# A four-layer modulated-convolution and adapter kernel: each engine's instructions of a step are written in another order

## What is computed

```python
def cond(x, style, weights, biases, mod_w, mod_b):   # four convolutions, three taps each
    for i, typ in enumerate(('same', 'upsample', 'same', 'downsample')):
        s = style @ mod_w[i].T + mod_b[i]
        weight = SCALE * w * s[:, None, :, None]                      # per sample
        weight = weight * lax.rsqrt(jnp.sum(weight * weight, axis=(2, 3)) + EPS)[:, :, None, None]
        x = conv(x, weight) + b                                       # with a blur where sampled
```

## The kernel before

| piece (function) | TensorE tiles | fed by |
|---|---|---|
| filter halves (`pe_halves`) | ps<-gu_hi,mid_hi | DVE `gu_lo` |
| first convolution (`pe_first`, one per sample q) | ps<-x_hi,first_hi | ACT `x_hi` L381, DVE `x_lo` L626 |
| filter (`pe_filter`) | ps<-fb_hi,up_hi | ACT `fb_hi` L371, DVE `fb_lo` L620 |
| folded convolution (`pe_conv`, one per sample) | ps<-xp_hi,filt | the filter, ACT/DVE `filt`, and two transfers per sample that shift it to other partitions (L322, L323) |
| transposes of y (`pe_transpose_y`) | ps<-ident,y_nat | ACT `y_nat` |
| projection (`pe_project`, L1409) | ps<-proj,y_f | ACT `y_f` |
| big product in halves (`pe_ffn`, not in layer 0) | ps<-w_hi,y_hi | ACT `y_hi`, DVE `y_lo` |
| transpose of z (`pe_project_T`, L1429), tail (`pe_tail`) | ps<-ident,z_sb; ps<-tail_hi,zt_hi | DVE `dve_route`; ACT/DVE `zt_hi`, `zt_lo` L1391 |

## Time and profile before

### The profile page before, as it was taken

One profiled execution on the slowest core, in us unless ns is written; L12 is line 12 of the kernel. 1 busy time (PEld: TensorE's weight loads), 2 busy tenths in 40 slices (PEclk: granted clock), 3 DMA queues, 4 the chain that ended last, 5 costly groups with the idle time before them and its releaser, 6 DMA issues.

```text
span 2215.3 us, 28460 instructions
## 1 busy us (share of the span) xinstructions
PE 1924.8 (87%) x9806; PEld 1579.7 (71%) x9806; DVE 906.0 (41%) x2626; ACT 635.7 (29%) x1161; POOL 82.4 (4%) x140
## 2 busy tenths in 40 slices
PE   1877888866899999998589999999988999999977
PEld 1666666655777778777478888888776788877755
DVE  4334444454333333334444344434554333333234
ACT  0033444422332332221433222222143333332200
POOL 0000000000000000000000000000000000000000
PEclk9979999986999999998689999999988999999975
DMA  6144546432322333223522221222132222222226
GB/s 106 46 93 106 144 102 146 114 86 68 70 67 53 78 78 78 66 57 71 113 46 74 74 54 56 74 74 54 49 119 46 74 74 74 74 74 73 64 86 246
DMA packets 248777, 182.99 MB, mean 83 GB/s; under 512 B 197688, under 2 KB 207960, under 8 KB 248734
## 3 DMA queue, kind: packets, MB, share of 16 engines
q1 hardware_dynamic: 212878, 169.77, 29.8%
q10 hardware_dynamic: 31360, 10.56, 2.0%
q0 software_dynamic: 4496, 2.12, 1.1%
HBM read 108.99 MB, written 44.04 MB: 69 GB/s over the span
## 4 chain that ended last, share of the span: by engine, by line
PE 69%; issue 10%; DVE 9%; ACT 5%; DMA 3%; ACTq 2%; SPq 1%; DVEq 0%; POOL 0%; POOLq 0%
PE ps L789 56%; PE ps L1409 3%; PE ps L916 2%; PE ps L868 2%; ACT x_hi L381 2%; DVE w_lo L1163 1%; ACTq L1233 1%; DVE x_lo L626 1%; SPq L998 1%; DMA out_x<-raw 1%; DMA x_in<-in_L_ffn_kernel 1%; DMA raw<-in_x 1%; ACT w_hi L1056 1%; PE ps L1276 1%; ACT tail_hi L1306 1%
## 5 line engine op out<-in xcount | busy, mean ns | idle before, releaser
L789 PE MATMUL ps<-xp_hi,filt 128*128 128x512 f32 x1024 | 340.9, 415 | 15.4 <-DMA filt<-filt 15.4
L789 PE MATMUL ps<-w_hi,y_hi 128*128 128x512 f32 x768 | 316.9, 413 | 0.0
L789 PE MATMUL ps<-w_hi,y_lo 128*128 128x512 f32 x768 | 309.9, 404 | 0.0
L789 PE MATMUL ps<-w_lo,y_hi 128*128 128x512 f32 x768 | 308.9, 402 | 0.0
L789 PEld LDWEIGHTS ps<-xp_hi,filt 128*128 128x128 f32 x1024 | 192.3, 196 | 57.4 <-DMA filt<-filt 15.8
L789 PE MATMUL ps<-xp_lo,filt 128*128 128x512 f32 x512 | 205.5, 401 | 0.0
L643 DVE SCALAR_TENSOR_TENSOR filt<-ps,mods_pair,filt 128x256 fp32r<-128x256 f32 x128 | 56.1, 480 | 326.4 <-ACT filt L398 326.4
L789 PEld LDWEIGHTS ps<-w_lo,y_hi 128*128 128x128 f32 x768 | 148.2, 193 | 36.2
L398 ACT ACTIVATE filt<-ps,mods_pair 128x256 fp32r<-128x256 f32 x128 | 53.7, 471 | 411.8 <-PE ps L789 411.8
L789 PEld LDWEIGHTS ps<-w_hi,y_hi 128*128 128x128 f32 x768 | 148.9, 194 | 32.1
L789 PEld LDWEIGHTS ps<-w_hi,y_lo 128*128 128x128 f32 x768 | 148.3, 193 | 31.5
(11 more groups left out here) (315 smaller groups left out, 3271.3 us busy)
## 6 DMA issues: line engine op xcount, KB each, us to landing
x_in<-x_state SPq DMA_DIRECT2D x96, 256.0 KB, 4.0
x_res<-x_state SPq DMA_DIRECT2D x48, 512.0 KB, 3.9
x_state<-x_res SPq DMA_DIRECT2D x48, 512.0 KB, 2.9
filt<-filt SPq DMA_DIRECT2D x128, 128.0 KB, 2.7
filt<-filt SPq DMA_DIRECT2D x128, 96.0 KB, 2.4
raw<-in_x SPq DMA_DIRECT2D x16, 512.0 KB, 5.1
x_res<-in_x SPq DMA_DIRECT2D x16, 512.0 KB, 6.0
x_state<-raw SPq DMA_DIRECT2D x16, 512.0 KB, 5.1
```

Source lines behind the costliest of these rows:

```text
L789: ins = nc.tensor.matmul(out, st[x0], mv[x1], start=first and t == 0, stop=last and t == 2, **kw)
```

## The change

The same work is done; only its places in the engines' lists move, and the split of the matrix is done in halves. TensorE's step gets a version of its own for layer 0 (`pe_step_0`). The z transposes go to PSUM bank 6 instead of 7. The diff, cut:

```diff
         def sp_step(sp, l, i, j, more, load_next):
-            if l == 0 and j == 0:
-                load_kernel(sp, i)
             sp.dma_start(x_res[:, j, :], ...).then_inc(res_loaded[j], 16)
+            if more and load_next:
+                sp_load_x(sp, l, n + 3)
+            if l == 0 and more and j == 1:
+                load_kernel(sp, i + 1)
             if more:
                 sp_shift_filter(sp, l, n + 2)
-            if more and load_next:
-                sp_load_x(sp, l, n + 3)
...
         # ACT, layer 0: y_nat q0, x_hi, exp, fb_hi, half a kernel split, y_nat q1, filt, xp_hi q0, zt_hi, xp_hi q1
         # ACT, layers 1 to 3:
+            if l > 0 and more:
+                act_halves(act, l, n + 2, j)
                 act_split_x(act, l, n + 2, j)
             if l == 1 and j == 0:
                 split_mixed_act(act, i)
-            if more:
-                act_halves(act, l, n + 2, j)
...
         # DVE, layer 0, behind y_nat q0:
+                if more:
+                    dve_split_x(dve, l, n + 2, j, (0,))
                 dve_route(dve, l, n)
+                if more:
+                    dve_split_x(dve, l, n + 2, j, (1,))
+                    dve_halves(dve, l, n + 2, j)
+                if edges:
+                    dve_edge(dve, l, i + 1, 2)
+                if more:
+                    split_kernel_dve(dve, i, j)
...
+        def pe_step_0(pe, i, j, more, one_more):
+            pe_transpose_y(pe, l, n, one_more)
+            pe_conv(pe, l, n + 1, 0)
+            pe_edge(pe, l, i + 1, 1)
+            pe_project(pe, l, i, j)
+            pe_halves(pe, l, n + 2)
+            pe_edge(pe, l, i + 1, 2)
+            pe_conv(pe, l, n + 1, 1)
+            pe_filter(pe, l, n + 2)
+            pe_edge(pe, l, i + 1, 3)
+            pe_first(pe, l, n + 2, 0)
+            pe_project_T(pe, l, i, j)
+            pe_first(pe, l, n + 2, 1)
+            pe_edge(pe, l, i + 1, 4)
+            pe_tail(pe, l, i, j)
...
         def pe_step(pe, l, i, j, more, one_more):   # layers 1 to 3
+            pe_transpose_y, pe_conv 0, pe_edge 1, pe_conv 1, pe_halves, pe_edge 2, pe_project, pe_ffn 0,
+            pe_first 0, pe_edge 3, pe_first 1, pe_filter, pe_edge 4, pe_project_T, pe_ffn 1, pe_tail
...
-        def split_kernel_dve(dve, e):
-            dve.wait_ge(s["kernel_act"], e + 1)
+        def split_kernel_dve(dve, e, half):
+            dve.wait_ge(s["kernel_act"], 2 * e + half + 1)
```

More of the change, by code:

```diff
@@ L424, in act_step @@
             if l == 0 and j == 0 and not more:
-                split_kernel_act(act, i)
+                for half in range(2):
+                    split_kernel_act(act, i, half)
             if more:
@@ L621, in dve_halves, with dve_split_x @@
                                                ALU.mult, ALU.subtract).then_inc(s["dve_b"], 1)
-        def dve_split_x(dve, l, k, par):
-            for q in range(2):
+        def dve_split_x(dve, l, k, par, samples=(0, 1)):
+            for q in samples:
                 dve.wait_ge(s["act_x"], smp(l, k, q))
@@ L725, in dve_step @@
             if l == 0 and j == 0 and nxt:
-                split_kernel_dve(dve, i)
-                dve.wait_ge(s["kernel_dve"], 9)
+                for half in range(2):
+                    split_kernel_dve(dve, i, half)
+                dve.wait_ge(s["kernel_dve"], 2 * GROUPS + 1)
             if nxt:
@@ L743, in dve_step @@
-            if more:
[L744 to L748, removed]
-            if more:
[L750 to L755, removed]
+            if l > 0:
+                if more:
+                    dve_halves(dve, l, n + 2, j)
+                if edges:
+                    dve_edge(dve, l, i + 1, 2)
+                if more:
+                    dve_split_x(dve, l, n + 2, j)
+                if l == 1 and j == 0:
+                    split_mixed_dve(dve, i)
+                if nxt and j == 0:
+                    dve_prep_transposed(dve, l + 1)
+                dve_route(dve, l, n)
@@ new lines, in dve_step @@
+            if more and l == 0:
+                dve_filter(dve, l, n + 2, j)
+            if more:
+                if l == 0 and edges:
+                    dve_edge(dve, l, i + 1, 3)
+                dve_first(dve, l, n + 2, 0, j)
+            if l == 0 and nxt and j == 0:
+                dve_prep_transposed(dve, l + 1)
+            if l == 0:
+                dve_tail_in(dve, l, n)
+            if more:
+                if l > 0 and edges:
+                    dve_edge(dve, l, i + 1, 3)
+                dve_first(dve, l, n + 2, 1, j)
+                if l > 0:
@@ L929, in pe_step @@
                 pe_edge(pe, l, i + 1, 1)
[L930 to L933, removed]
+            pe.wait_ge(s["act_f"], whole_y(l, n, 1))
+            pe.wait_ge(s["dve_o"], pid(l, n) + 1)
+            pe_project(pe, l, i, j)
+            if edges:
+                pe.wait_ge(s["dve_e"], edge_count(l, i + 1, 4))
+            if more:
+                pe_halves(pe, l, n + 2)
+            if edges:
+                pe_edge(pe, l, i + 1, 2)
             if one_more:
                 pe_conv(pe, l, n + 1, 1)
+            if nxt and j == 0:
+                pe_prep_forms(pe, l + 1)
             if edges:
[L937 to L942, removed]
+                pe.wait_ge(s["dve_e"], edge_count(l, i + 1, 6))
             if more:
-                pe_halves(pe, l, n + 2)
+                pe_filter(pe, l, n + 2)
             if one_more:
@@ L951, in pe_step @@
                 pe_first(pe, l, n + 2, 0)
-                if l == 0:
-                    pe_filter(pe, l, n + 2)
+            if nxt and j == 0:
+                pe_prep_s(pe, l + 1)
+            if nxt and j == 1:
+                pe_prep_bias(pe, l + 1, 0)
+            pe_project_T(pe, l, i, j)
+            if more:
                 pe_first(pe, l, n + 2, 1)
@@ L970, in pe_step @@
                 pe_prep_bias(pe, l + 1, 0)
-            if more and l > 0:
+            if more:
+                pe_first(pe, l, n + 2, 0)
+            if edges:
+                pe_edge(pe, l, i + 1, 3)
+            if more:
+                pe_first(pe, l, n + 2, 1)
+            if edges:
+                pe.wait_ge(s["dve_e"], edge_count(l, i + 1, 6))
+            if more:
                 pe_filter(pe, l, n + 2)
+            if edges:
+                pe_edge(pe, l, i + 1, 4)
             pe_project_T(pe, l, i, j)
@@ L1332, in act_tail_in @@
             for b, rows in enumerate(ZT_ROWS[l]):
-                last = nc.scalar.activation(zt_hi[0:rows, b, :], ps[0:rows, 7, P * b:P * b + P], ACT.Copy)
+                last = nc.scalar.activation(zt_hi[0:rows, b, :], ps[0:rows, 6, P * b:P * b + P], ACT.Copy)
             last.then_inc(s["act_zt"], 1)
@@ L1390, in dve_tail_in @@
             for b, rows in enumerate(ZT_ROWS[l]):
-                last = v.tensor_tensor(zt_lo[0:rows, b, :], ps[0:rows, 7, P * b:P * b + P], f(zt_hi[0:rows, b, :]), ALU.subtract)
+                last = v.tensor_tensor(zt_lo[0:rows, b, :], ps[0:rows, 6, P * b:P * b + P], f(zt_hi[0:rows, b, :]), ALU.subtract)
             last.then_inc(s["dve_zt"], 1)
@@ L1428, in pe_project_T @@
             for b in range(len(ZT_ROWS[l])):
-                last = nc.tensor.transpose(ps[:, 7, P * b:P * b + P], z_sb[:, P * b:P * b + P], ident[:])
+                last = nc.tensor.transpose(ps[:, 6, P * b:P * b + P], z_sb[:, P * b:P * b + P], ident[:])
             last.then_inc(s["pe_zt"], 1)
```

107 lines of the change are left out of this document (66 added, 41 removed).

## The result

| | before | after |
|---|---|---|
| median of the executions | 2214.97 us | 2154.57 us |
| lowest to highest | 2214.12 to 2216.78 | 2152.19 to 2158.10 |
| the profile's span | 2215.3 us | 2150.5 us |

The ratio is 0.9728 (95% interval 0.9711 to 0.9744): 60 us, 2.7% faster.

The account below looks back on a forecast made before the run. TensorE, busy 87% of the span, was taken as the bound, leaving its idle time and clock to win. Terms of -45 - 7 + 16 - 17.5 + 4 = -49.5 us from 2217.0 gave 2168 us, range 2146 to 2192.

Parts of the forecast that it names:

- Layer 0, what goes: Layer 0's loop: four TensorE waits for DVE vanish with their drains, 9.1 us a group, 64 us in seven.
- Layer 0, what comes: Layer 0's loop: new waits at tail, transposes and filter shifts add 19 us, 3 to 33 by the bounds.
- Filter: Layer 0's steps: the filter starts about when DVE has its input; 0 taken, bounds 0 to 0.5 a step.
- Tail in j = 1: Layer 0, step j = 1: 2.1 us of ACT and DVE work against 1.5 of TensorE work, wait 0.6 us.
- Transposes behind j = 0: Layer 0: the next step's transposes wait 0.4 us for the last edge operation on DVE.
- Shifts: Layer 0, j = 1: filter shifts queued behind x and the matrix come 2.0 us late, six times, 12 us.
- The rival that the queue holds nothing back: Layer 0: filter shifts come in time and the clock stays up, 12 + 8 us less, 2148; chance 0.14.
- The clock in layer 0: Layer 0's loop: the loss to half-speed stretches stays as before, no change, bounds -8 to +10 us.
- Layer 0 to layer 1: Between the layers: the matrix's last eighth, loaded earlier and split in halves, saves 7 us, bounds 4 and 8.
- Layer 1: Layer 1's loop: a new 5.5 us projection wait makes it 16 us longer, clock 4 us more.
- Layers 2 and 3: Loops of layers 2 and 3: the first convolution's wait is covered, 17.5 us shorter, bounds 10 and 18.

Follow-up runs that it names:

- e8: Changed kernel, but TensorE's second convolution in layer 0 stands ahead of the filter halves and edge stage 2 again; 2182.0 us on the result's scale, ratio 0.9851.
- e4: Changed kernel, but layer 0's z transpose stands behind sample 1's first convolution and edge stage 4, right ahead of the tail; 2174.4 us on the result's scale, ratio 0.9817.
- e2: Changed kernel, but in layer 0, step j = 1, SP issues the matrix's eighth behind the filter shifts; 2143.2 us on the result's scale, ratio 0.9676.
- e7: Changed kernel, but in layer 0's last group DVE starts on the matrix's last eighth only after ACT did both halves; 2157.15 us, one execution, no ratio.
- e5: Changed kernel, but in layer 1, j = 0, ACT and DVE split the mixture's rows first, the wait staying at the projection; 2134.6 us on the result's scale, ratio 0.9637.
- e1: Changed kernel, but layer 1's TensorE wait for the split mixture rows stands at the tail, not the projection; 2096.5 us on the result's scale, ratio 0.9465.
- e6: Changed kernel with layer 1's mixture wait at the tail and the matrix's eighths, save the last, behind the filter shifts; 2085.8 us on the result's scale, ratio 0.9417.
- e3: Changed kernel, but all four engines' lists in the steps of layers 1 to 3 are those before the change; 2147.9 us on the result's scale, ratio 0.9697.

## Why the prediction was right, and where it was off

The span's difference is 64.8 us, the sum said 49.5. Of these 15.3 us, 4.4 are where the two profiled executions lie about their medians; by the medians the change gained 60.4.

- **Layer 0, what goes.** Right. The 64.0 us of waits left 19.2. Undone alone, the filter's cover is worth 27 us (e8) and the z transpose's 20 us (e4), net of the shift waits that go with either. The covers of the waits for `e_y` and `x_lo`, 20.9 us together, were not undone alone; that their waits are gone is read from the trace. The z transposes' other PSUM bank was not undone alone either.
- **Layer 0, what comes.** Right in kind and size. Filter 0 (summed 0). Tail in j = 1 0.5 (0.6). Transposes behind j = 0 0.16 (0.4). Shifts six times 1.5 to 2.1, 11.0 us (12), ended with the matrix's place (e2). The sum put 1.8 us between the issue of x and its first packet; the traces of both kernels show 1.4 (242.33 to 243.77 before, 214.25 to 215.69 after). The rival that the queue holds nothing back is out. The groups behind the first are 37.2 to 37.8 us (37.8).
- **The clock in layer 0: the term that was mis-sized.** The step reads "a wait of 2 us next to the short transposes replaces 2.5 us split by a transpose: no change, -8 to +10". Of the 59.4 us, 44.8 are waits and about 4 the drains, as summed; the other 10.6 are clock, which the sum put at nothing. The kernel before has six stretches at 1.2 GHz in this loop besides the one at the first wait, 27.3 us in all: the four that the prediction counted, and two in the first step, at 169.3 and 176.1, that it missed. Each begins within 1.2 us of the end of a wait: one at the filter, three at the z transpose (`e_y`), two at the tail. The change has none of these waits but 0.5 us at the tail, and none of the six stretches. The step compared one pair of waits (2.5 us, split by a transpose) with one new wait of 2 us and expected the same falls. The runs show that the covered waits matter: put back one at a time, at 1.5 to 1.8 us at the filter (e8) or 1.7 to 1.9 us at the tail (e4), they bring stretches with them, eight and six. The six waits of 1.5 to 2.1 us for the shifts, at the start of a step, bring none in the change. So the length of the single wait does not decide it. Whether its place does or the sum of waits near it (19.2 us in the change's loop, 32.4 in e4's, 31.6 in e8's), the runs don't tell. This is the largest part of the 15 us between sum and result.
- **Layer 0 to layer 1.** Right: 20.26 us from the last group's start to the forms' restart became 13.28, 7.0 for the 7 summed. e2 and e7 show two of its parts, the eighth's date and the halves (0.9 for 1.0); how much the earlier load gave in all was not undone alone. The rest of the passage varied by some us with the clock: 79.9 us in the change's profile, 81.3 to 84.4 in the others'.
- **Layer 1.** Right: seven waits of 5.3 us (5.5) at the projection, ended by `tail_lo`. Less 22.75 us for what goes, that is +14.5 (16). The clock took +9 and not +4, inside its bounds of -2 to +10: before, the stretches at half clock were mostly 3.4 us, now they are six of 6.8 and one of 10.2. e5 and e1 show that the stretch follows the wait. The prediction took the wait as a given of the change. The text in front of it gives as the reason that the same counter guards the loaded projection; that is wrong. The kernel has two counters: `mixed_loaded` guards the loaded rows that the projection reads, `mixed_dve` the split of the tail rows, which on TensorE the tail alone reads. So the wait for the second could be moved, as e1 did.
- **Layers 2 and 3.** -15.5 for -17.5. Layer 2 gave 9.3 (8.75), layer 3 only 6.2: in two of its groups a new stretch of 3.4 us at half clock takes 1.5 us each (57.06 and 57.08 us against 55.53).
- **Not foreseen**: 2.4 us ahead of the first loop, where the prologue took 141 to 145 us in all runs, which is chance, and 1.8 us in other places.

Terms, measured less summed: -14.4 in layer 0's loop, -2.2 in the passage, +3.5 in layer 1, +2.0 in layers 2 and 3 and -4.2 elsewhere are the -15.3 between sum and result.

## What to carry to other kernels

When work is moved ahead, its waits move with it and everything behind them on that engine is held: before moving a piece, split its waits by what each operation reads, and leave each with its reader. Cover for a chain over two other engines is found by counting what stands between producer and consumer in the waiting engine's own list; a piece of 3 us put there was worth 27 us here. And in a queue that is served in order, what is urgent and small goes ahead of what is large and has a step of time, and the last transfer of a series may need another place than the rest.

## What the runs showed of the hardware

- Idle time had a second price. Behind a wait of 5.3 us the projection ran at near 1.2 GHz and the wait cost 8.2 us; behind 3.0 us, 4.6 or more (e1, e5). In layer 0 waits of 1.5 to 1.9 us at the filter or the tail had stretches of mostly 3.4 us behind some of them (e4, e8), and waits of 1.5 to 2.1 us at the start of a step had none (the change).
- The clock also fell with no idle time ahead. In layer 3 of the change TensorE is busy throughout 1805 to 1815 at 0.99, and then:

```profile
1805.00:1815.00 10.00, 10.00 (x58) 8.38 (x57) 5.41 (x19) 5.27 (x10) 2.43 (x4) 0.99 0.31 107
1815.40:1818.80 3.40, 3.40 (x11) 2.67 (x10) 0.34 (x2) 0.00 (x0) 0.00 (x0) 0.59 0.38 101
```

  The same two groups of layer 3 show it in the profiles of the change and of e1, e2, e4, e5, e6 and e8, three groups do in e7, and none does in e3, whose layer 3 has the old order with its wait of 1.2 us. It cost 3 us in all. Ahead of the fall stand edge stage 2 and the projection, both of short matmuls, but they stand there in the groups without a fall too, so its cause is open: the Trainium skill (TensorE: Matmul & The Clock Gate, section "What's actually happening") ties the half clock to an idle engine, which agrees with the waits of e1 and e5 and not with these two rows.
- TensorE's busy time moves with the clock: in layer 0's loop 248.4 us in the change and 257.1 in e4, for the same matmuls. A busy share says nothing of work done unless the granted clock stands beside it.
